# Relative values of a unit placed between its turned scores and its first value sums, and picks done as transposes into the PSUM ring

## What is computed

```python
scores = jnp.einsum('bhld,bhrd->bhlr', Q, K) * scale
scores = scores + jnp.einsum('bhld,lrd->bhlr', Q, rel_k)
attn = jax.nn.softmax(scores, axis=-1)
out = jnp.einsum('bhlr,bhrd->bhld', attn, V)
out = out + jnp.einsum('bhlr,lrd->bhld', attn, rel_v)
```

## Time and profile before

| | us |
|---|---|
| median of 3 runs | 3481.03 (3480.51 to 3482.59) |
| the profiled execution, its own time | 3486.41 |
| its span | 3485.2 |
| PE busy in the span | 3231.7 (93%) |
| DVE, ACT, POOL busy | 2768.4, 2633.0, 2205.2 |

### The profile page before, as it was taken

How to read it: one execution, slowest core, us unless ns; L and a number is a source line. 1 busy time by engine, 2 the same in 40 slices (tenths; PEclk the granted TensorE clock), 3 DMA queues, 4 the chain that set the end, 5 groups by cost and what they waited for, 6 DMA issues and landing times. The chain is left out here.

```text
span 3485.2 us, 166713 instructions
## 1 busy us (share of the span) xinstructions
PE 3231.7 (93%) x65430; PEld 2576.3 (74%) x65430; DVE 2768.4 (79%) x7853; ACT 2633.0 (76%) x5852; POOL 2205.2 (63%) x2407
## 2 busy tenths in 40 slices
PE   7589999999999999999999999999999996999990
PEld 4357777777777777777777777777777785579980
DVE  6478888888888888888888888888888885534443
ACT  3288888888888888888888888888888883244440
POOL 0167777777777777777777777777777764700006
PEclk9779999999999999999999999999999997589995
DMA  6666666666666666666666666666666664712224
GB/s 211 227 228 213 220 218 221 218 221 221 215 222 220 222 221 223 221 221 223 219 219 221 222 222 219 224 219 222 218 218 223 219 212 161 236 53 66 64 61 143
DMA packets 356377, 701.33 MB, mean 201 GB/s; under 512 B 59545, under 2 KB 168706, under 8 KB 355346
## 3 DMA queue, kind: packets, MB, share of 16 engines
q1 hardware_dynamic: 349458, 673.92, 59.7%
q0 software_dynamic: 6144, 16.79, 1.5%
HBM read 343.02 MB, written 347.46 MB: 198 GB/s over the span
## 5 line engine op out<-in xcount | busy, mean ns | idle before, releaser
L851 POOL TENSOR_TENSOR pt_near<-pt_full,pt_near 128x512 f16<-128x512 f32 (+3 forms) x1984 | 1844.7, 959 | 662.9 <-DVE pt_near L1160 662.8
L1067 ACT ACTIVATE pt_full<-pb,exp_bias 128x512 f32<-128x512 f32 x2048 | 1315.1, 689 | 324.5 <-PE pb L946 240.4
L999 PEld LDWEIGHTS pb<-pt_near,table_high 128*128 128x128 f16 x18432 | 794.7, 97 | 153.4 <-issue 117.2
L999 PE MATMUL pb<-pt_near,table_high 128*128 128x64 f16 (+6 forms) x18432 | 884.7, 187 | 17.0 <-DVE rel_out L1193 16.5
L1140 DVE TENSOR_REDUCE part_max<-pb 128x1 f32<-128x512 f32 (+3 forms) x1376 | 770.5, 574 | 114.7 <-PE pb L904 114.0
L999 PE MATMUL pb<-pt_near,table_low 128*128 128x64 f16 (+6 forms) x9216 | 851.5, 187 | 0.0
L999 PEld LDWEIGHTS pb<-pt_near,table_low 128*128 128x128 f16 x9216 | 772.7, 96 | 0.1
L1136 DVE CUSTOM_DVE_ANT_0 near_sum<-pb,skewed 128x512 bf16<-128x512 f32 (+3 forms) x1216 | 675.5, 571 | 114.6 <-PE pb L904 86.2
L938 PE MATMUL pb<-ident,skewed 128*128 128x128 f32 x3840 | 625.0, 286 | 6.9 <-ACT q_max L1091 4.8
L1160 DVE CAST pt_near<-pt_full 128x512 f16<-128x512 f32 (+3 forms) x1280 | 542.4, 474 | 0.3 <-PE pb L972 0.3
L972 PE MATMUL pb<-v_head,pt_near 128*128 128x33 f16 x13440 | 501.0, 178 | 2.3 <-POOL pt_near L851 2.2
(11 more groups left out here) (183 smaller groups left out, 4087.6 us busy)
## 6 DMA issues: line engine op xcount, KB each, us to landing
skewed<-rel_scratch SPq DMA_DIRECT2D x256, 576.0 KB, 5.5
rel_scratch<-rel SPq DMA_DIRECT2D x416, 319.5 KB, 3.4
rel_scratch<-rel SPq DMA_DIRECT2D x320, 320.0 KB, 2.8
skewed<-rel_scratch SPq DMA_DIRECT2D x64, 512.0 KB, 4.5
skewed<-rel_scratch SPq DMA_DIRECT2D x64, 448.0 KB, 4.4
k_stack<-planes_scratch SPq DMA_DIRECT2D x192, 96.0 KB, 4.8
planes_scratch<-planes SPq DMA_DIRECT2D x64, 256.0 KB, 2.3
rel_scratch<-rel SPq DMA_DIRECT2D x64, 256.0 KB, 2.7
```

What stands on the lines that cost most here:

```text
L851: ins = nc.gpsimd.tensor_tensor(pt_piece(c, 1, a, z, near), pt_full[e][:, (a - 4 * g) * P:(z - 4 * g) * P], pt_piece(c, 0, a, z, near), AL ...
L999: ins = nc.tensor.matmul(acc[:, c0:c1, :], keep[table][:, w:w + P], pt_near[half][:, part, c0:c1, d - M_LO, a * SHIFTS:(a + 1) * SHIFTS], ...
L1067: nc.scalar.activation(pt_full[e][:, :], x_ps[e % 2][:, :], ACT.Exp, bias=exp_bias[:, 0:1]).then_inc(s_exp, 1)
```

## The change

Four edits:

1. `first` becomes 4: with j other than 0, all four quarters of `rel_values` stand between `rel_products` and the first two `values`, that is ahead of T1. None stands at the end of the step. With j equal to 0 nothing moves.
2. `pick_values` becomes eight fp32 transposes (PE, identity as the constant operand) into two banks of the ring, four units in each; the ring's order gets two more items in these steps. DVE sums over the eight shifts straight from the ring (`sum_values`, two `tensor_reduce`) into a new SBUF buffer `rel_sum`.
3. The two last operations of a half (`output`) go from DVE to POOL, one step later (`LAG_O` is one more), and SP stores the half in an earlier step of the following half (`i == 2`).
4. The constant `pick` and its eight `affine_select` on POOL at the start go; waits on `s_o` for the bank of `s_ps` go with it.

```diff
-LAG_O = LAG_SEL + 1
+LAG_O = LAG_SEL + 2
+PICK_BANKS = 2
+PICK_C = HALF_C // PICK_BANKS
...
-            ("scores", k - LAG_S, 1), ("scores", k - LAG_S, 3), ("max", k - LAG_A, 0)]
+            ("scores", k - LAG_S, 1), ("scores", k - LAG_S, 3), ("max", k - LAG_A, 0)] + \
+        [("pick", k - LAG_SEL, n) for n in range(PICK_BANKS) if (k - LAG_SEL) % HALF_C == 0]
...
-                if i == HALF_C - 1 and h >= 0 and exists(it, h * HALF_C):
+                if i == 2 and h >= 0 and exists(it, h * HALF_C):
...
+            def output(it, h):
+
+                pool.wait_ge(s_rp, PICK_BANKS * (h + 1))
+                pool.wait_ge(s_or, it * HALF_STEP + h + 1)
...
+                nc.gpsimd.tensor_tensor(out[h % 2][:, :, :], rel_sum[h % 2][:, :, :], o_sum[h % 2][:, :, :],
+                                        ALU.add).then_inc(s_o1, 1)
+                pool.wait_ge(s_o1, it * HALF_STEP + h + 1)
+                nc.gpsimd.tensor_tensor(out[h % 2][:, :, :], out[h % 2][:, :, :],
+                                        inv_sum[h % 2][:, :, :].to_broadcast([P, HALF_C, DK]), ALU.mult).then_inc(s_o, 1)
...
-                ins = nc.tensor.matmul(s_ps[:, i * DK:(i + 1) * DK],
-                                       rel_out[:, i, :, :].rearrange("p a b -> p (a b)"), keep["pick"][:, :],
-                                       start=True, stop=True)
...
+                wait_bank(it, "pick", h * HALF_C, n)
+                for i in range(PICK_C):
+                    ins = nc.tensor.transpose(bank_of("pick", h * HALF_C, n)[:, i * P:(i + 1) * P],
+                                              rel_out[:, PICK_C * n + i, :, :].rearrange("p a b -> p (a b)"), keep["ident"][:, :])
+                ins.then_inc(s_sel, 1)
...
-                first = 2 if rel_on and j else 0
+                first = 4 if rel_on and j else 0
...
+            def sum_values(it, h, n):
+
+                dve.wait_ge(s_sel, PICK_BANKS * h + n + 1)
                 if h >= 2:
+                    dve.wait_ge(s_o, it * HALF_STEP + h - 1)
+                src = bank_of("pick", h * HALF_C, n)[:, :].rearrange("p (c s d) -> p c d s", c=PICK_C, s=SHIFTS)
+                nc.vector.tensor_reduce(rel_sum[h % 2][:, PICK_C * n:PICK_C * (n + 1), :], src,
+                                        axis=AX.X, op=ALU.add).then_inc(s_rp, 1)
```

More of the change, by code:

```diff
@@ L360, in _ @@
         def _(pool):
-            ident, pick, shift_mask = keep["ident"], keep["pick"], keep["shift_mask"]
+            ident, shift_mask = keep["ident"], keep["shift_mask"]
             nc.gpsimd.memset(keep["blank"][:, :], 0.0).then_inc(s_id, 1)
@@ L364, in _ @@
             nc.gpsimd.memset(ident[:, :], 0.0).then_inc(s_pre, 1)
-            nc.gpsimd.memset(pick[:, :], 0.0).then_inc(s_pre, 1)
             nc.gpsimd.memset(shift_mask[:, :], 1.0).then_inc(s_pre, 1)
-            pool.wait_ge(s_pre, 3)
+            pool.wait_ge(s_pre, 2)
             nc.gpsimd.affine_select(out=ident[:, :], in_=ident[:, :], compare_op=ALU.not_equal,
                                     fill=1.0, base=0, pattern=[[-1, P]], channel_multiplier=1).then_inc(s_id, 1)
-            for j in range(SHIFTS):
-                if j:
-                    pool.wait_ge(s_id, j + 2)
-                nc.gpsimd.affine_select(out=pick[:, :], in_=pick[:, :], compare_op=ALU.not_equal, fill=1.0,
-                                        base=-DK * j, pattern=[[-1, DK]], channel_multiplier=1).then_inc(s_id, 1)
             nc.gpsimd.affine_select(out=shift_mask[:, :], in_=shift_mask[:, :], compare_op=ALU.is_ge, fill=0.0,
                                     base=-DK * (SHIFTS - 1), pattern=[[DK, SHIFTS]], channel_multiplier=1).then_inc(s_id, 1)
-            pool.wait_ge(s_id, SHIFTS + 3)
+            pool.wait_ge(s_id, 3)
             nc.gpsimd.affine_select(out=shift_mask[:, :], in_=shift_mask[:, :], compare_op=ALU.is_ge, fill=0.0,
@@ L499, in _ @@
         def _(pe):
-            pe.wait_ge(s_id, SHIFTS + 4)
+            pe.wait_ge(s_id, 4)
             pe.wait_ge(s_w, 16 * weights)
@@ L583, in attend @@
         rel_out = sb("rel_out", [P, HALF_C, SHIFT_GROUPS, SHIFTS])
+        rel_sum = [sb(f"rel_sum{i}", [P, HALF_C, DK]) for i in range(2)]
         part_max = sb("part_max", [P, 2, 8])
@@ L590, in attend @@
         score_ps, x_ps, r_ps = psum[:BANKS], psum[BANKS:BANKS + 2], psum[7]
-        o_ps, s_ps = psum[6][:, 0:HALF_C * VW], psum[6][:, HALF_C * VW:HALF_C * (VW + DK)]
+        o_ps = psum[6][:, 0:HALF_C * VW]
         s_qin = [sem(f"b_queries{i}") for i in range(2)]
@@ L620, in attend @@
         s_rle = sem("b_rel_values_on_chip")
-        s_sel = sem("b_rel_values_picked")
+        s_sel = sem("b_rel_values_turned")
+        s_rp = sem("b_rel_values_summed")
         s_o1 = sem("b_out_steps")
@@ L670, in wait_bank @@
                     nc.tensor.wait_ge(s_ge, it * (2 * STEP) + 2 * u + m + 1)
+                elif last == "pick":
+                    nc.tensor.wait_ge(s_rp, PICK_BANKS * (u // HALF_C) + m + 1)
                 else:
@@ L854, in low_part @@
                 ins.then_inc(s_lo, 1)
+            def output(it, h):
+                pool.wait_ge(s_rp, PICK_BANKS * (h + 1))
+                pool.wait_ge(s_or, it * HALF_STEP + h + 1)
+                if h >= 2:
+                    pool.wait_ge(s_ow[h % 2], 16 * (h // 2))
+                nc.gpsimd.tensor_tensor(out[h % 2][:, :, :], rel_sum[h % 2][:, :, :], o_sum[h % 2][:, :, :],
[3 more added lines that the diff above has]
+                                        inv_sum[h % 2][:, :, :].to_broadcast([P, HALF_C, DK]), ALU.mult).then_inc(s_o, 1)
             def step(it, k):
@@ L860, in step @@
                         low_part(it, u, e)
+                h, j = half_at(k, LAG_O)
+                if j == 0 and h >= 0 and exists(it, h * HALF_C):
+                    output(it, h)
                 if V0 <= k % NB < V0 + len(V_STAGES) // 2 and exists(it, (k // NB + 1) * NB):
@@ L1004, in rel_values, with pick_values @@
                     ins.then_inc(s_rl, 1)
-            def pick_values(it, h, i):
-                if i == 0:
+            def pick_values(it, h, n):
+                if n == 0:
                     pe.wait_ge(s_rle, it * (2 * HALF_STEP) + 2 * h + 2)
-                    if h:
-                        pe.wait_ge(s_o, it * HALF_STEP + h)
-                ins = nc.tensor.matmul(s_ps[:, i * DK:(i + 1) * DK],
-                                       rel_out[:, i, :, :].rearrange("p a b -> p (a b)"), keep["pick"][:, :],
-                                       start=True, stop=True)
-                if i == HALF_C - 1:
-                    ins.then_inc(s_sel, 1)
+                wait_bank(it, "pick", h * HALF_C, n)
[3 more added lines that the diff above has]
+                ins.then_inc(s_sel, 1)
             def step(it, k):
@@ L1044, in step @@
                 if h >= 0 and j == 0 and exists(it, h * HALF_C):
-                    for i in range(HALF_C):
-                        pick_values(it, h, i)
+                    for n in range(PICK_BANKS):
+                        pick_values(it, h, n)
             pipeline(pe, step)
@@ L1187, in mask_values @@
                 if part == 0 and h:
-                    dve.wait_ge(s_sel, it * HALF_STEP + h)
+                    dve.wait_ge(s_sel, PICK_BANKS * h)
                 half_a = SHIFT_GROUPS // 2
@@ L1218, in step @@
                 adding, turning = exists(it, a), exists(it, t)
-                h, j = half_at(k, LAG_O)
+                h, j = half_at(k, LAG_SEL + 1)
                 if j == 0 and h >= 0 and exists(it, h * HALF_C):
-                    output(it, h)
+                    for n in range(PICK_BANKS):
+                        sum_values(it, h, n)
                 h, j = half_at(k, LAG_PV + HALF_C)
@@ L1840, in program @@
             keep["table_low"] = sbi("table_low", [P, TABLE_N * DK], FP16)
-            keep["pick"] = sbi("pick_dim", [P, DK])
             keep["blank"] = sbi("blank", [CLEAR, D])
```

11 lines of the change are left out of this document (removed).

## The result

The changed kernel takes 3706.11 us in the median of 4 runs (3698.88 to 3708.51), the one before 3480.79 (4 runs, 3480.51 to 3482.59): a ratio of 1.0644 with the interval 1.0628 to 1.066. The profiled execution took 3698.88 us, the fastest of the four, with a span of 3697.1. The forecast was 3685, in the range 3650 to 3800.

What follows compares the result with a forecast made beforehand. It took a 5.01 us loop through PE and ACT, coinciding with PE's work, as the bound; 322 - 87 - 37 + 5 + 1 = +204 gave 3690 profiled, 3685 as the runs' median, range 3650 to 3800.

Steps and rivals of the forecast that it cites:

- What bounds the kernel: Plain attention step: PE's work and the loop T0, T1, ACT's exponentials, q_max copy, next T0 coincide at 5.01 us.
- The group, +322: Second group of relative values, moved ahead of T1: 0.73 us longer in each of 441 steps, +322 us.
- Absorbed, -87: PE's waits for DVE in the same loop: 2.9 us per 16 steps absorbed, in 30 patterns, -87 us.
- The picks, -37: Pick steps, bound by PE: eight transposes take 1.1 us instead of 1.7, -0.6 in each of 62, -37 us.
- DVE's sums and POOL, +5 and 0: Two DVE sums a half, 0.68 us each: +5 (0 to 50); POOL's output operations: nothing, at most 31 us.
- The clock, 1.00 throughout: Trace of the changed kernel: PE's granted clock expected to stay at 1.00 throughout.
- The rival: Clock falls to the lower level in a quarter of the moved steps: +220 more, 3905 us; chance 0.09.
- Costed at nothing: POOL's two output operations a half, at most 1.5 us together: cost nothing, at most 31 x 1 us.

Runs made afterwards that it cites:

- the order alone: The kernel before with both groups of relative values ahead of T1 in the moved steps, picks, sums and output as before: 3733.81 us, ratio 1.0721.
- the run with the gap filled: The changed kernel plus eight unread identity products at the end of every moved step: 3687.54 us, ratio 1.0593.
- the picks alone: The changed kernel with its order set back (two quarters ahead of T1, two at the step's end): 3463.19 us, ratio 0.9942.

## Why the prediction was right

*What bounds the kernel.* Right, and shown: the loop T0, T1, exponentials, copy set the plain step, not PE's 97.7%. Cutting the group left the steps at 5.01, moving it made them 5.73 (5.74 predicted), moving 15 of its 27 matmuls 5.43 (5.42 expected).

*The group, +322.* Right: 0.71 to 0.77 in the steps without DVE waits, against 0.73.

*Absorbed, -87.* Right in kind, too large: 2.0 to 2.1 us in a pattern instead of 2.9, some 25 us over 30 patterns. The waits were read in one pattern of 85.13 us, whose 5.43 step with its 0.42 wait is rare (the medians add up to 84.68, and that block's is 5.01). The rest of the shortfall isn't the order's. With the order alone some 2.4 us a pattern are absorbed; what the changed kernel lacks against that is the 0.21 of B 4 and the 0.10 of B 1, told of under the sums. A pattern is to be checked against the others before its small waits are multiplied by 30.

*The picks, -37.* Right in sign, too small: 0.88 a step, 54 us. I took 0.136 us each from the five transposes of T1, with the step to other products behind them, and 1.7 for the old picks; eight in a row with more transposes behind them take 0.91 to the next T0, 0.114 each, and the old ones took 1.79. The 54 us are what the two pick steps give at full clock; 12.6 of them go to the falls in B 0.

*DVE's sums and POOL, +5 and 0.* Nearly right for the sums, too small for POOL. The sums take 0.64 each. L901 waits 13.1 us in all, in single waits of up to 0.5 where at most 0.2 was predicted; 4 us of it lengthen A 1 and some 3 us B 1 (5.31 against 5.21 with the order alone). In B 4 PE's wait for the mask's product, which DVE makes, is

```profile
1029.17 0.11 PEld L1011 LDWEIGHTS pb<-pt_near,table_high 128*128 128x128 f16 x2 [0.53 <-DVE rel_out L1203]
```

against 0.32 with the order alone, and the step 0.21 longer, 6.5 us in all. That this is `output` on POOL is argued: with the order undone B 4 is back at its 5.58 as soon as `output` stands elsewhere. So together they cost some 14 us, and not 5. With the order undone they cost some 6 to 10 us (A 1 up by 0.19 in the mean, 0.32 with `output` two steps later) and, for POOL, some 30 (B 4 to B 6); of the latter the longer loop covers most. "Costed at nothing" named POOL's wait for DVE as its cover, and that was an average over a pattern; at the place where `v_part` stands there was no slack.

*The clock, 1.00 throughout.* Wrong. The rival came true in small, in a place I hadn't named: not in the moved steps but in the pick step behind the last of them, 10 times, 12.6 us by its rows and 15 to 19 by the run with the gap filled. By its size it is nearly the forecast's error, since 3706 less 19 is 3687.5, against 3685; but the other terms were off too.

By positions the account closes: 30 halves A at +4.16 and 31 halves B at +2.25 are 194.6 us, the clock 12.6, the means of A 1 above its medians 4, together 211, where the stretch from the T0 of unit 16 to that of unit 504, which holds just these halves, has grown by 209.5. The forecast had +204 against 212.5 in the profiled execution. Too much absorbed (+25, of which some 10 are POOL's and DVE's) and too little for the picks (-17) nearly cancelled, the clock added 12.6 and A 1's long waits 4, less the 5 expected for them, and behind the attention 5 us came back; some 6 us of these sums stay unassigned. That the sum lands within 8.5 us (21 in the medians, +225) is in part luck; the term that carries it, the group in the loop, is not.

## What to carry to other kernels

When an engine is busy 97% of the time and the page calls it the bound, follow one step from the engine out through the others and back: if that loop closes in just the step's length, the engine's work that lies outside the loop is free and the same work inside it costs its full duration, 0.73 us here in the 11 steps of a pattern that had no other wait in the loop, less in the three that had. The quick experiment is to take the work away and not to move it: no gain means that it was cover. And before a small extra operation is put on an engine with "slack", look at what stands behind it in the one step where it goes; the same 1.2 us on GpSimd cost some 30 us in one place of the pattern, and two steps later the kernel was 21 us faster.

## What the hardware showed that I had not expected

Work that nobody needs made a kernel faster: 3528 matmuls in TensorE's gaps took 3706 to 3687.5. With the gaps of 0.68 us left empty the granted clock fell to half in ten of 62 pick steps, for 3.4 us each, just where TensorE was the bound; with them filled it fell in none. The version with the second group cut away had such falls in 15 steps, the kernel that kept the group in none of its steady part, and it ended 13 us slower.

VectorE's rounded copies of two buffers take 1.18 to 1.76 us when GpSimd's operations run beside them, at 1383.73 and 1388.78 of the version with the picks alone, against 0.76 in the plain steps of the kernel before:

```profile
1383.73 1.18 DVE L1170 CAST pt_near<-pt_full 128x512 f16<-128x512 f32 x2
```

```profile
1445.34 0.76 DVE L1160 CAST pt_near<-pt_full 128x512 f16<-128x512 f32 x2
```

The kernel before has both kinds already. Of its 768 copies of this shape, taken one by one, the 262 with no GpSimd operation beside them take 0.41 to 0.42 us, and the 88 that lie wholly beside one 0.63 to 0.96.

The Trainium skill, page "Perfetto Trace Analysis", section "Optimizing Scalar/DVE Operations", warns of this: "Remember GPSIMD and DVE share an SBUF read port", so that moving operations from one to the other might not help. The trace agrees in this place. But over the whole kernel the copies are no slower with the picks alone, 0.515 us in the mean against 0.523 before; how much of the 30 us is the slower copy in B 4 and B 5 and how much POOL's own lateness, no run here separates.
